# FFN1's last stage: small gating products before H's fourth block, low-rank updates added in H's own banks, two final additions on ACT and POOL

## What is computed

```python
H = jnp.einsum('btd,od->bto', x, W) + b
z = jnp.einsum('btd,dr->btr', x, A)                     # r = 32
anchors = jnp.arange(N_GRAM - 1, T, N_GRAM)             # every second token
H_slice = H[:, anchors, :E]                             # E = 8 experts
delta_slice = jnp.einsum('bar,er->bae', z[:, anchors], LiMEs)
H_scale = jnp.maximum(jnp.max(jnp.abs(H_slice)), EPS)   # over all tokens
d_scale = jnp.maximum(jnp.max(jnp.abs(delta_slice)), EPS)
logits = (0.5 * H_slice / H_scale + 0.5 * delta_slice / d_scale)
probs = jax.nn.softmax(logits, axis=-1)
mask = jax.nn.sigmoid((probs - second_largest(probs)) / 0.5)
weights = probs * mask / (sum(probs * mask) + 1e-9)
p_mix = jnp.einsum('bte,er->btr', repeat(weights, 2), LiMEs)
delta = jnp.einsum('btr,ro->bto', z * p_mix, Bmat) * 0.5
out = x + H + delta                                     # x here: the residual
```

## Time and profile before

| what | us |
|---|---|
| median of 3 runs (1169.13 to 1169.9) | 1169.54 |
| the profiled execution | 1169.32 |
| its span in the trace | 1167.5 |

### The profile page before, as it was taken

The page is one execution under the profiler, slowest core; times in us unless marked ns, Lnnn a source line. Parts: engine busy times, 40 slices in busy tenths (PEclk is TensorE's granted clock), DMA queues, the critical chain, the costliest instruction groups (busy, mean ns, idle before and its releaser), DMA issues.

```text
span 1167.5 us, 15309 instructions
## 1 busy us (share of the span) xinstructions
PE 1127.2 (97%) x5478; PEld 905.2 (78%) x5478; DVE 560.2 (48%) x1021; ACT 513.9 (44%) x1390; POOL 371.1 (32%) x250
## 2 busy tenths in 40 slices
PE   6999999999999999987999999999999999999997
PEld 4787787787787688865888888888888888888774
DVE  5374364364368443388433524335243352433665
ACT  5474374374277332333623516235162351623631
POOL 3151052053043353555412404124041240412440
PEclk9999999999999999998999999999999999999998
DMA  8011011010000221110111101101011110110001
GB/s 251 14 41 28 1 40 27 0 45 9 0 19 1 91 90 36 55 37 1 55 36 36 54 0 54 36 36 54 0 54 36 36 54 0 39 36 1 13 4 72
DMA packets 22646, 43.55 MB, mean 37 GB/s; under 512 B 14069, under 2 KB 14325, under 8 KB 19925
## 3 DMA queue, kind: packets, MB, share of 16 engines
q1 hardware_dynamic: 22612, 43.12, 11.3%
HBM read 41.02 MB, written 2.10 MB: 37 GB/s over the span
## 4 chain that ended last, share of the span: by engine, by line
PE 87%; DVE 6%; ACT 2%; POOL 2%; issue 2%; DMA 0%; SPq 0%; DVEq 0%
PE work L482 14%; PE work L484 14%; PE work L483 14%; PE work L544 8%; PE yb L482 5%; PE yb L484 5%; PE yb L483 5%; PE pt L554 4%; PE ov L484 3%; PE ov L482 3%; PE ov L483 3%; PE pt L484 3%; PE pt L483 3%; PE pt L482 3%; DVE minus_mean L1408 1%
## 5 line engine op out<-in xcount | busy, mean ns | idle before, releaser
L1150 POOL TENSOR_TENSOR prob<-prob,exp_rcp 128x512 f32<-128x512 f32 (+1 forms) x96 | 127.3, 1326 | 586.7 <-DVE exp_rcp L1331 586.7
L968 ACT ACTIVATE prob<-work,neg_max 128x128 f32<-128x128 f32 (+1 forms) x384 | 149.2, 407 | 69.1 <-DVE neg_max L1355 68.4
L482 PE MATMUL work<-xT_hi,q_hi 128*128 128x512 f32 x416 | 169.1, 407 | 5.1 <-DVE xT_lo L1420 5.1
L484 PE MATMUL work<-xT_hi,q_lo 128*128 128x512 f32 x416 | 165.1, 397 | 0.0
L483 PE MATMUL work<-xT_lo,q_hi 128*128 128x512 f32 x416 | 164.8, 396 | 0.0
L544 PE MATMUL work<-kT,qT 128*128 128x128 f32 (+1 forms) x768 | 128.2, 310 | 1.0 <-DVE qT L1265 0.9
L544 PEld LDWEIGHTS work<-kT,qT 128*128 128x128 f32 (+1 forms) x768 | 114.1, 191 | 14.2 <-issue 1.6
L921 ACT ACTIVATE pT_hi<-pt 128x512 fp32r<-128x512 f32 x128 | 73.8, 603 | 84.0 <-PE pt L554 83.5
L1388 DVE TENSOR_TENSOR oT_lo<-ov,oT_hi 32x128 fp32r<-32x128 f32 (+2 forms) x160 | 67.4, 421 | 78.3 <-ACT oT_hi L927 76.9
L1355 DVE TENSOR_REDUCE neg_max<-work 128x4 f32<-128x512 f32 (+1 forms) x96 | 83.0, 865 | 40.1 <-PE work L544 38.2
L482 PE MATMUL yb<-o_hi,oT_hi 128*128 128x512 f32 x224 | 94.0, 419 | 4.8 <-DVE oT_lo L1388 4.7
(11 more groups left out here) (189 smaller groups left out, 2113.2 us busy)
## 6 DMA issues: line engine op xcount, KB each, us to landing
q_raw<-in_l_q SPq DMA_DIRECT2D x8, 1024.0 KB, 4.8
o_raw<-in_l_o SPq DMA_DIRECT2D x8, 1024.0 KB, 4.8
kv_raw<-in_l_kv SPq DMA_DIRECT2D x8, 515.0 KB, 3.3
o_raw<-in_l_o SPq DMA_DIRECT2D x4, 768.0 KB, 4.3
q_raw<-in_l_q SPq DMA_DIRECT2D x16, 144.0 KB, 2.5
qT<-in_ctxT SPq DMA_DIRECT2D x4, 512.0 KB, 6.8
x<-in_x SPq DMA_DIRECT2D x2, 1024.0 KB, 11.4
q_raw<-in_up SPq DMA_DIRECT2D x2, 1024.0 KB, 6.2
```

Of the source, the lines that this page charges most:

```text
L482: pe.matmul(dst, l_hi, r_hi, start=first and k == 0, stop=False)
L484: mm = pe.matmul(dst, l_lo, r_hi, start=False, stop=last and k == n - 1)
L968: e = act.activation(prob[:, i % 2, g * L.keys:(g + 1) * L.keys], s[:, g, :], ACT.Exp, bias=neg_max[:, i % 2, g:g + 1], accum_out=exp_sum[ ...
L1150: pool.tensor_tensor(p, p, exp_rcp[:, b % 2, :].unsqueeze(2).broadcast_to([P, G, L.keys]), ALU.mult)\
```

## The change

Five edits at FFN1's end:

- PE makes the small products right after z, ahead of H4 instead of behind it. H6 is cut in two, with the transposes of the weights between its halves, and the mixing product stands ahead of H7.
- `add_h(4)` to `add_h(7)` go. For blocks 4 to 7 the correction is accumulated in the bank that holds H (`start=False`), and one addition to `x` takes both.
- The corrections are made in the order 6, 7, 4, 5, 0, 1, 2, 3, and so the second half of `zp3` is made first.
- Blocks 6 and 7: ACT copies the bank to `moved` in SBUF, POOL adds it to `x`. The other six stay with DVE, in the order 4, 5, 0, 1, 2, 3.
- SP writes the blocks in the order 4, 5, 0, 6, 7, 1, 2, 3.

```diff
+        DELTAS = (6, 7, 4, 5, 0, 1, 2, 3)
+        BY_DVE = DELTAS[2:]
+        def delta_bank(b):
+            return work[:, L1.last_bank["h", b], :] if b >= 4 else (ov[:, :], pt[:, 1, :])[b % 2]
...
@@ sync @@
-            for b in range(NB):
-                sp.wait_ge(f1.done, b + 1)
+            for n, b in enumerate(DELTAS[2:5]):
+                sp.wait_ge(f1.done, n + 1)
+                sp.dma_start(out[b], x[:, b, :]).then_inc(out_stored, 16)
+            for n, b in enumerate(DELTAS[:2]):
+                sp.wait_ge(f1.moved_done, n + 1)
+                sp.dma_start(out[b], x[:, b, :]).then_inc(out_stored, 16)
+            for n, b in enumerate(DELTAS[5:]):
+                sp.wait_ge(f1.done, n + 4)
                 sp.dma_start(out[b], x[:, b, :]).then_inc(out_stored, 16)
...
@@ tensor @@
             z_half(1)
-            big_h(4)
...
             mm.then_inc(f1.small, 1)
-            for b in range(5, NB):
-                big_h(b)
+            big_h(4)
+            big_h(5)
+            big_h(6, (0, 1))
...
             mm.then_inc(f1.wT, 1)
+            big_h(6, (2, 3))
             pe.wait_ge(f1.wT_evac, 1)
             pe.matmul(yb[0:RANK, :], limes[:, :], wT[:, :], start=True, stop=True).then_inc(f1.pmix, 1)
+            big_h(7)
             pe.wait_ge(f1.b_lo, 1)
-            for b in range(NB):
-                pe.wait_ge(f1.zp_again, 1 if b < 4 else 2)
-                pe.wait_ge(f1.zp_lo, 1 if b < 4 else 2)
-                if b >= 2:
-                    pe.wait_ge(f1.done, b - 1)
-                pe.matmul(d2[b % 2], zp3[:, b * P:(b + 1) * P], b3[:, :], start=True, stop=True)\
+            for b in DELTAS:
+                pe.wait_ge(f1.zp_again, 1 if b >= 4 else 2)
+                pe.wait_ge(f1.zp_lo, 1 if b >= 4 else 2)
+                if b in (2, 3):
+                    pe.wait_ge(f1.done, BY_DVE.index(b - 2) + 1)
+                pe.matmul(delta_bank(b), zp3[:, b * P:(b + 1) * P], b3[:, :], start=b < 4, stop=True)\
                     .then_inc(f1.delta, 1)
...
@@ scalar @@
-            for half in range(2):
-                act.wait_ge(f1.zp, half + 1)
+            for n, half in enumerate((1, 0)):
+                act.wait_ge(f1.zp, n + 1)
...
+            for n, b in enumerate(DELTAS[:2]):
+                act.wait_ge(f1.delta, n + 1)
+                act.activation(moved[:, n, :], delta_bank(b), ACT.Copy).then_inc(f1.moved, 1)
@@ gpsimd @@
+            for n, b in enumerate(DELTAS[:2]):
+                pool.wait_ge(f1.moved, n + 1)
+                pool.tensor_tensor(x[:, b, :], x[:, b, :], moved[:, n, :], ALU.add).then_inc(f1.moved_done, 1)
@@ vector @@
             evac_z(1)
-            add_h(4)
...
-            add_h(5)
...
-            add_h(6)
...
-            add_h(7)
...
-            for half in range(2):
+            for half in (1, 0):
...
-            for b in range(NB):
-                dve.wait_ge(f1.delta, b + 1)
-                dve.wait_ge(f1.H_added, b + 1)
-                dve.tensor_tensor(x[:, b, :], x[:, b, :], d2[b % 2], ALU.add).then_inc(f1.done, 1)
+            for b in BY_DVE:
+                dve.wait_ge(f1.delta, DELTAS.index(b) + 1)
+                if b < 4:
+                    dve.wait_ge(f1.H_added, b + 1)
+                else:
+                    dve.wait_ge(f1.b_added, b + 1)
+                dve.tensor_tensor(x[:, b, :], x[:, b, :], delta_bank(b), ALU.add).then_inc(f1.done, 1)
```

More of the change, by code:

```diff
@@ L218, in __init__ @@
         self.delta = sem(f"{prefix}_delta")
+        self.moved = sem(f"{prefix}_moved")
         self.done = sem(f"{prefix}_done")
+        self.moved_done = sem(f"{prefix}_moved_done")
         self.b_added = sem(f"{prefix}_b_added")
@@ L305, in build_program @@
             b_bc = sb("b_bc", [P, HID], stack=st)
+            moved = sb("moved", [P, 2, HID], stack=st)
             AC = HALF // P
@@ L324, in build_program @@
         logitsT = relu[:, :, :].rearrange("p a t -> p (a t)")
-        d2 = [ov[:, :], pt[:, 1, :]]
+        DELTAS = (6, 7, 4, 5, 0, 1, 2, 3)
+        BY_DVE = DELTAS[2:]
+        def delta_bank(b):
+            return work[:, L1.last_bank["h", b], :] if b >= 4 else (ov[:, :], pt[:, 1, :])[b % 2]
         def o_buf(L, part, b):
@@ L672, in fc1, with big_h @@
                     .then_inc(f0.lin, 1)
-            def big_h(b):
+            def big_h(b, ks=range(KT)):
                 if b == 0:
                     pe.wait_ge(q_lo_done, F1_W + 1)
[L678 to L683, removed]
+                if ks[0] == 0:
+                    pe.wait_ge(N[3].lo, b + 1)
+                    L1.wait_bank(pe, S1, L1.kv_heads - 1, "h", b, last=True, drained=drained_by)
+                mm = product(work[:, L1.last_bank["h", b], :],
+                             [((xT_hi[:, k, b * P:(b + 1) * P], xT_lo[:, k, b * P:(b + 1) * P]),
+                               (q_hi[:, k * HID:(k + 1) * HID], q_lo[:, k * HID:(k + 1) * HID]))
+                              for k in ks], ks[0] == 0, b < 4)
+                if b < 4:
+                    mm.then_inc(f1.H, 1)
             def attention(L, S, norm):
@@ L1608, in _ @@
                                          op0=ALU.mult, op1=ALU.mult).then_inc(f1.zp, 1)
-            for half in range(2):
-                dve.wait_ge(f1.zp_hi, half + 1)
+            for n, half in enumerate((1, 0)):
+                dve.wait_ge(f1.zp_hi, n + 1)
                 at = slice(half * HALF, (half + 1) * HALF)
```

## The result

| what | us |
|---|---|
| before, median of 8 (1168.86 to 1170.13) | 1169.34 |
| the change, median of 8 (1165.34 to 1167.75) | 1166.01 |
| ratio, with its 95% interval | 0.9972 (0.9961 to 0.9983) |
| the change once more, median of 6 (1165.19 to 1167.34) | 1165.53 |
| ratio, with its 95% interval | 0.9969 (0.9956 to 0.9981) |

The change is faster by 0.3%, and 1166.0 lies 0.3 us from the forecast. The profile shows that this closeness is partly luck: one step was wrong by 0.7 us, another by 0.6, and some executions pay for something that the forecast had set aside.

The account below looks back on a forecast made before the run. At the end, needless additions delay the PE chain to the mixing product, then writing at 385 GB/s bounds the tail. Span 1152.13 + 10.74 + 1.43 = 1164.30, 3.20 us less (2.68 + 0.52); median 1166.3 us, range 1165.0 to 1167.6.

Parts of the forecast that it names:

- Small products: On PE ahead of H4, waiting for DVE's `zT`: start at 1140.34 in place of 1142.21, PE standing still 0.84 us.
- POOL's readiness: POOL's library change after its bias additions, ahead of the reduction: taken as 6.93 us, so POOL starts the reduction at 1142.94.
- POOL is ready sooner: Rival, chance 0.25: library change under 6.3 us, so PE sets the mixing product's end at 1151.49; time 1165.7 us.
- Q: End of PE's mixing product: forecast 1152.13, 2.68 us earlier than before.
- The chain without the three additions: From POOL's reduction to the end of the weights: 8.62 us less three waits (0.77, 0.83, 0.87) gives 6.15 us.
- the 0.64 us of waiting at the transposes: PE, done with 30 products of H at 1148.51, was to wait 0.64 us for the weights before transposing at 1149.15.
- H7 behind the mixing product: H7's twelve products beside `zp3`; DVE's first addition ends at Q + 4.40 (before Q + 4.12), a cost of 0.28 us.
- Writing: Output of eight blocks at 385 GB/s without gaps, from Q + 5.29 to Q + 10.74 in place of 11.26.
- The tail follows the last addition: Rival, chance 0.04: the end keeps its 3.07 us behind the last addition; gain 4.80 us, time 1164.7 us.
- The 1.43 us behind the data: Time from the end of the written data to the span's end, kept at 1.43 us in the forecast sum.
- The clock: Rival, chance 0.05: PE's clock falls to 0.50 at the new standstills, H4 to H7 cost 11.0 us more; 1177 us.
- the 1.00 at 24 to 25 us: Argument against the clock rival: PE was busy for 0.09 us in that window and its clock stayed at 1.00.

Follow-up runs that it names:

- the repeat: The changed kernel run again, unedited, for a second profile; median of 6 1165.53 us, ratio 0.9969, profiled execution 1165.31 us.
- these three runs: The changed kernel with 6, 12 or 24 unused DVE steps zeroing columns of `pad` behind DVE's last addition; 1162.60, 1164.36 and 1162.32 us, one run each.
- 24 steps: The changed kernel with twenty-four unused DVE steps, zeroing columns of `pad`, behind DVE's last addition; 1162.32 us, one run.

## Why the prediction was right, and where not

All by the repeat, whose clock was undisturbed.

- *Small products.* 1140.34 forecast, 1140.35 measured, 0.88 us of standstill for 0.84. Right.
- *POOL's readiness.* Wrong. The step that failed is "The nearest row is the change back, 6.93 us ... I take that". The first change takes 5.75, so POOL was ready 0.1 us ahead of its data, and the reduction came 0.36 us behind DVE's row maximum. The rival *POOL is ready sooner* is what happened, and its threshold (6.3 us) and its Q (1151.49; measured 1151.43) hold. 0.70 us.
- *The chain without the three additions.* 6.15 us forecast, 1148.10 - 1141.83 = 6.27 measured. Right; of the 0.64 us of waiting at the transposes nothing is left, since POOL was early.
- *H7 behind the mixing product.* First addition Q + 4.40 forecast, Q + 4.42 measured. Right.
- *Writing.* Start Q + 5.29 forecast, Q + 5.31 measured; end Q + 10.74 forecast, Q + 10.84 measured; no gap, full windows at about 385 GB/s. *The tail follows the last addition* fell with the eight additions on DVE.
- *The 1.43 us behind the data.* Taken over from before without a reason, and wrong: it held 0.6 us of an engine that a code fetch had delayed. Net of what lies outside of the span, 0.21 us.
- *The clock.* The rival was given 0.05 and a price of 11.0 us. The mechanism is real: 0.88 us of standstill was followed by 0.59 and 0.55 in one trace, against the reasoning from the end of the kernel before, where the clock first fell 1.2 us or more into the idle time. The other half of that reasoning, the 1.00 at 24 to 25 us, held for the trace of before and not for this one: PE was idle for 1.85 us up to 25.5, and from 26.2 to 29.6 us the clock was at 0.50.

```profile
27.00:28.00 1.00, 1.00 (x4) 0.56 (x3) 0.93 (x5) 0.00 (x0) 0.55 (x1) 0.50 0.74 161
```

  The rival's price was far too high, because the clock came back after 3.4 us: Q is 1153.85 there, `zT` was 0.86 later, so 1153.85 - 1151.43 - 0.86 = 1.56 us. Of 14 executions, two are more than 2 us above the lowest of their set; in the profiled one about 0.5 us of that comes from the fall at 26 us.

The sum: the repeat's execution took 4.01 us less than before's (1169.32 - 1165.31), forecast 3.20. The 0.81 between is 0.70 (POOL) - 0.10 (writing) + 0.60 (trailing engine) - 0.39 (outside of the span). The first set's median then lay 0.3 us from the forecast, because half of that set's executions were slower than this one by 0.7 us or more. One had a fallen clock. Two of the other three have the repeat's mean clock, 0.996, which 3.4 us more at 0.50 would lower by 0.0015; what held them isn't shown. The rival's 1165.7 lies 0.3 and 0.2 us from the two medians, the forecast's 1166.3 0.3 and 0.8.

## What to carry to other kernels

A price taken over from "the nearest row" should be measured where it carries the sum: loading a library and going back to the built-in code are two prices, 5.75 and about 7 us. Where the writing limits the end, as here, an earlier first block or fewer gaps move it; engines that help with the last blocks didn't. And a step put early in front of the bottleneck engine should come with work that fills the wait: three products ahead of the small ones, for a standstill of 0.7 us less, brought Q 0.3 us sooner and left none of five executions far above the others. The median was 0.6 us lower, though the intervals of the two ratios overlap.

## What the runs showed that was not expected

- PE's clock can fall behind a standstill as short as 0.88 us in one execution and stay at 1.00 behind the same one in another.
- One 8 KB code fetch, among 2.1 MB of output, went with one DMA engine 0.5 to 0.75 us late in all five traces that have it among the blocks, and that engine set the span's end.
- The unused `pad` tile is declared in the middle of the SBUF tiles, so that all tiles declared behind it lie 24, 48 or 96 bytes further on. In these three runs `zT` came 2.30, 1.27 and 3.32 us sooner than in the repeat, a lead that grows over the whole span (with 24 steps, medians over DVE's instructions: 1.0 us late at 50 to 100 us, 1.0 early around 600, 3.3 at the end). In the other traces the lead or lag against the repeat is constant to 0.1 us, but for one step of at most 0.6 us in three of them: in the first profile at the fall of the clock at 26 us, in two others between 520 and 550 us, where the clock's stretches at 0.50 lie otherwise than in the repeat. Products got shorter, for instance in the output projection (line, operands, count, busy us, mean ns, the repeat and the 24 unused steps):

```profile
L496 PE MATMUL yb<-o_lo,oT_hi 128*128 128x512 f32 x224 | 88.6, 396 | 0.0
```

```profile
L497 PE MATMUL yb<-o_lo,oT_hi 128*128 128x512 f32 x224 | 87.5, 391 | 0.0
```

  Whether the tiles' places or something else in these kernels did it isn't told apart, and with one run each the sizes are uncertain. If it holds, it is worth as much as the change under study.
